# Summing edges with the one-hots as weights, two groups side by side in TensorE's column halves, then placing the sums

## The reference, cut to what matters

```
h = relu(layernorm(x))
agg = segment_sum(edge_attr, dst, 12500)          # 200000 x 48 -> 12500 x 48
z1 = silu(concat(h, agg) @ W1 + b1)               # 176 -> 256
z2 = silu(z1 @ W2 + b2)                           # 256 -> 256
out = x + h + z2 @ W3 + b3                        # 256 -> 128
```

## Time and profile before

| | |
|---|---|
| median of 3 runs | 367.58 us (367.41 to 370.16) |
| the profiled execution's own time | 369.57 us |
| its span, first to last instruction | 367.8 us |
| PE busy | 347.2 us (94%) |
| PE weight loads busy | 327.8 us (89%) |
| DVE busy | 260.8 us (71%) |
| ACT busy | 203.1 us (55%) |
| POOL busy | 32.6 us (9%) |
| data moved | 52.96 MB, 144 GB/s on average |

### The profile page before, as it was taken

How to read it: one execution, slowest core, us unless ns; L and a number is a source line. 1 busy time by engine, 2 the same in 40 slices (tenths; PEclk the granted TensorE clock), 3 DMA queues, 4 the chain that set the end, 5 groups by cost and what they waited for, 6 DMA issues and landing times.

```text
span 367.8 us, 11752 instructions
## 1 busy us (share of the span) xinstructions
PE 347.2 (94%) x4336; PEld 327.8 (89%) x4337; DVE 260.8 (71%) x630; ACT 203.1 (55%) x377; POOL 32.6 (9%) x44
## 2 busy tenths in 40 slices
PE   1488999999999999999999999999999999999995
PEld 1387999999999999999999999999999999999994
DVE  6864866976687667866796669766876688666652
ACT  7543466555655566456645565556555654566471
POOL 4011101110111001110111011101110011101100
PEclk9996999999999999999999999999999999999999
DMA  4953756454555455455635554545554555551111
GB/s 136 295 158 83 219 152 177 131 167 134 175 134 165 127 173 168 131 138 172 182 115 152 165 174 123 169 133 175 137 163 127 172 153 149 138 170 28 27 27 47
DMA packets 78757, 52.96 MB, mean 144 GB/s; under 512 B 2482, under 2 KB 78348, under 8 KB 78738
## 3 DMA queue, kind: packets, MB, share of 16 engines
q1 hardware_dynamic: 78738, 52.70, 50.3%
HBM read 46.29 MB, written 6.40 MB: 143 GB/s over the span
## 4 chain that ended last, share of the span: by engine, by line
PE 93%; DVE 4%; issue 2%; POOL 1%; ACTq 0%; DVEq 0%; POOLq 0%; ACT 0%
PE agg_ps L836 41%; PE z L899 14%; PE z L880 7%; PE z L888 6%; PE z L882 6%; PE z L869 3%; PE z L864 3%; PE z L870 3%; PE z L865 3%; PE z L866 3%; PE tp L849 3%; DVE farthest L522 1%; PE z L774 1%; DVE window L505 0%; DVE rel_rows L518 0%
## 5 line engine op out<-in xcount | busy, mean ns | idle before, releaser
L836 PEld LDWEIGHTS agg_ps<-onehot,raw 128*48 128x48 f32 x3128 | 147.8, 128 | 7.3 <-issue 3.6
L836 PE MATMUL agg_ps<-onehot,raw 128*48 128x42 f32 x3128 | 151.1, 217 | 3.3 <-issue 3.3
L714 DVE TENSOR_TENSOR out_t<-z,resid 112x512 f32<-112x512 f32 (+1 forms) x28 | 19.4, 692 | 84.6 <-PE z L899 84.6
L558 DVE TENSOR_TENSOR onehot<-window,rel 128x1176 f32<-128x1176 f32 (+1 forms) x56 | 76.9, 1375 | 0.7
L425 ACT ACTIVATE xn<-x_t,nmr,rstd 112x128 f32<-112x128 f32 (+1 forms) x112 | 46.2, 483 | 36.6 <-DVE nmr L550 29.8
L899 PEld LDWEIGHTS z<-w,h 128*112 128x112 f32 (+1 forms) x448 | 51.7, 176 | 5.3 <-issue 4.5
L377 POOL TENSOR_TENSOR rstd<-vareps,minus_half 112x4 f32<-112x4 f32 (+1 forms) x28 | 28.2, 1008 | 312.0 <-DVE vareps L542 312.0
L899 PE MATMUL z<-w,h 128*112 128x128 f32 (+1 forms) x448 | 54.4, 274 | 0.9 <-ACT h L446 0.9
L446 ACT ACTIVATE h<-z,b2c 128x448 f32<-128x448 f32 (+1 forms) x56 | 32.4, 631 | 26.5 <-PE z L888 26.5
L880 PE MATMUL z<-h_hi,w_hi 128*128 128x448 f32 (+1 forms) x112 | 43.5, 389 | 0.0
L385 ACT ACTIVATE agg_ps<-zeros 48x512 f32<-48x512 f32 x28 | 16.5, 592 | 45.4 <-DVE agg_carry L668 45.4
(11 more groups left out here) (89 smaller groups left out, 341.4 us busy)
## 6 DMA issues: line engine op xcount, KB each, us to landing
raw<-in_edge_attr_dram SPq DMA_DIRECT2D x55, 672.0 KB, 4.6
x_t<-in_x_dram SPq DMA_DIRECT2D x27, 224.0 KB, 2.9
out_dram<-out_t SPq DMA_DIRECT2D x27, 224.0 KB, 2.5
dst_rows<-in_dst_dram SPq DMA_DIRECT2D x1, 768.0 KB
raw<-in_edge_attr_dram SPq DMA_DIRECT2D x1, 480.0 KB, 4.0
out_t<-in_L_gnn_W_dram SPq DMA_DIRECT2D x1, 256.0 KB, 7.0
x_t<-in_x_dram SPq DMA_DIRECT2D x1, 192.0 KB
out_dram<-out_t SPq DMA_DIRECT2D x1, 192.0 KB
```

The source lines that it names most:

```text
L558: return dve.tensor_tensor(onehot[:, slot, 0:n * PER, :], window[:, :].unsqueeze(1).broadcast_to([P, n * PER, WINDOW]), cols.unsqueeze(2). ...
L836: mm = pe.matmul(banks[0:ED, bass.ds(offsets[k], WINDOW)], raw[0:rows, slot, k, j, :], onehot[0:rows, slot, k * PER + j, :], start=False, ...
```

## The change

The edges' sums are made in two stages.

First `sum_tile` multiplies with the **one-hot as weights** (128 x 42) and the **edges moving** (128 x 48). Its result is a group's 42 x 48 sums at a fixed place of one PSUM bank, `stage`: groups of even number on partitions 0 to 41, those of odd number on 64 to 105 (`tile_position=(0, 0)` and `(0, 64)`), 7 pairs of groups next to each other. No offset is needed for it. ScalarE copies the bank to SBUF (`stage_sums`, 106 x 336).

Then `place_batch` puts each group in its place: one fp32 multiplication with the staged sums (106 x 48) as weights and 42 columns of the identity as the moving operand, added into `agg_ps` at the group's offset, two pairs of load and matmul for each group. A batch is shifted by 3 groups against the tile: batch b places groups 14b-3 to 14b+10, so that the bank of tile b-1 is closed within it, and its offsets are read from entry 14b-3 on.

What goes with it: `stage` takes a bank, so that both layers now share one `z` (2 banks) in place of `z1` and `z2`, and `layer1` waits for `activate2` of the tile before, chunk by chunk. `layer2` is done chunk by chunk. TensorE's step becomes `layer1(i-1)`, `offsets_of(i+1)`, `sum_tile(i+1)`, `layer3(i-2)`, `transposes(i)`, `place_batch(i+1)`, `layer2(i-1)`. ScalarE's and VectorE's orders are rewritten, edges are loaded three tiles ahead into the same four slots, and one-hots are made two tiles ahead. The start is rearranged: the first entry of each group and the first 128 groups of `dst` are loaded ahead of the rest, tiles 0 and 1 are summed before the offsets of the other groups are known, and TensorE gets some matmuls of the identity whose results are not used.

The core of the diff:

```diff
-    LOOP_FIRST, LOOP_END = 4, 24
+    LOOP_FIRST, LOOP_END = 4, 22
+    WARM0, WARM1 = 10, 6
...
+        staged = sb("staged", [ROW2 + WINDOW, 2, PAIRS, ED])
...
-        z1 = ps("z1", [P, M, BANK])
-        z2 = ps("z2", [P, M, BANK])
+        stage = ps("stage", [P, BANK])
+        z = ps("z", [P, M, BANK])
...
             def step(i, parity):
-                if has(i, -2, NT):
-                    load_edges(i + 2, parity, 0)
+                if has(i, -3, NT):
+                    load_edges(i + 3, 1 - parity, 0)
...
+            def stage_sums(t, parity):
+
+                act.wait_ge(s_summed, 2 * t + 2)
+                if not isinstance(t, int) or t > 1:
+                    act.wait_ge(s_placed, t)
+                act.activation(staged[:, parity].rearrange("w k d -> w (k d)"), stage[0:ROW2 + WINDOW, 0:STAGED],
+                               ACT.Copy).then_inc(s_staged, 1)
...
             def step(i, parity):
                 if has(i, 1, NT):
                     relu(i - 1)
+                if isinstance(i, int) and i == 1:
+                    clear_carry(2)
+                if has(i, 1, NT):
+                    split_agg(i - 1)
                 if has(i, 1, NT - 2):
                     act.wait_ge(s_carried, i)
                     clear_bank(1 - parity)
-                if has(i, 1, NT):
-                    split_agg(i - 1)
-                if has(i, 0, NT):
-                    normalize(i, parity)
                 if has(i, 2, NT):
                     activate2(i - 2)
                 if has(i, 1, NT):
                     activate1(i - 1)
-
+                if has(i, 0, NT):
+                    normalize(i, parity)
+                if has(i, -1, NT):
+                    stage_sums(i + 1, 1 - parity)
...
-            def offsets_of(i):
-                count = sum(groups_of(i, half)[0] for half in range(2))
+            def batch_of(b):
+
+                t = isinstance(b, int)
+                first = 0 if t and b == 0 else -EARLY
+                last = sum(groups_of(b, half)[0] for half in range(2)) if t and b == NT - 1 else GPT - EARLY
+                return first, last
+
+            def offsets_of(b):
+                first, last = batch_of(b)
                 _, offsets = nc.values_load_multi_w_load_instructions(
-                    offset_row[0:1, bass.ds(i * GPT, count)], engines=[mybir.EngineType.PE],
+                    offset_row[0:1, bass.ds(b * GPT + first, last - first)], engines=[mybir.EngineType.PE],
...
+                    for j in range(PER):
+                        for side in range(2):
+                            half, k = divmod(2 * pair + side, HALF)
+                            if 2 * pair + side < total:
+                                rows = P if k < counts[half][1] else TAIL_P
+                                at = ROW2 * side
+                                mm = pe.matmul(stage[at:at + WINDOW, pair * ED:(pair + 1) * ED],
+                                               onehot[0:rows, 2 * parity + half, k * PER + j, :],
+                                               raw[0:rows, 2 * parity + half, k, j, :],
+                                               start=(pair == 0 and j == 0), stop=True, skip_group_check=True,
+                                               tile_position=(0, at))
...
+            def place_batch(b, parity, offsets):
+
+                first, last = batch_of(b)
+                pe.wait_ge(s_staged, b + 1)
+                wait(pe, s_clear, b + 1)
+                for offset, k in zip(offsets, range(first, last)):
+                    group = k % GPT
+                    at = ROW2 * (group % 2)
+                    mm = pe.matmul(banks[0:ED, bass.ds(offset, WINDOW)], staged[:, parity if k >= 0 else 1 - parity, group // 2, :],
+                                   ident[0:ROW2 + WINDOW, at:at + WINDOW],
+                                   start=False, stop=True, skip_group_check=True)
...
                 for m in range(M):
                     cols = slice(m * P, (m + 1) * P)
-                    pe.matmul(z1[:, m, 0:n], w1x_hi[:, cols], hT_hi[:, 0:n], start=True, stop=False)
...
+                    wait(pe, s_h2, M * (t - 1) + m + 1)
+                    pe.matmul(z[:, m, 0:n], w1x_hi[:, cols], hT_hi[:, 0:n], start=True, stop=False)
...
                     layer1(i - 1)
                 if has(i, -1, NT):
                     offsets = offsets_of(i + 1)
+                    sum_tile(i + 1, 1 - parity)
                 if has(i, 2, NT):
                     layer3(i - 2)
                 if has(i, 0, NT):
                     transposes(i, parity)
                 if has(i, -1, NT):
-                    sum_tile(i + 1, 1 - parity, offsets)
+                    place_batch(i + 1, 1 - parity, offsets)
                 if has(i, 1, NT):
                     layer2(i - 1)
 
-            sum_tile(0, 0, first_offsets)
+            pe.wait_ge(s_stage_clear, 1)
+            sum_tile(0, 0)
...
+            sum_tile(1, 1)
+            transposes(0, 0)
+            first_offsets = offsets_of(0)
+            offsets = offsets_of(1)
+            where_invalid(pe, mybir.EngineType.PE, general_path)
+            place_batch(0, 0, first_offsets)
+            place_batch(1, 1, offsets)
             pipeline(pe, step)
```

More of the change, by code:

```diff
@@ L113, in gnn_kernel @@
         centre_i = sb("centre_i", [P, ROWS], I32)
+        first_i = sb("first_i", [P, ROWS], I32)
         g = {n: sb("g_" + n, [P, ROWS]) for n in (
-            "base", "middle", "centre", "drift", "ok1", "ok2", "ok3", "valid", "invalid",
-            "tile", "tilet", "tile_half", "pair", "parity", "offset", "offset2", "offset3",
-            "at_centre", "instead", "placed", "shift")}
+            "base", "middle", "minus_middle", "centre", "tilet", "tile", "tile_half", "pair", "parity",
+            "begin", "in_tile", "at_centre", "other", "if_before", "if_behind", "from_centre",
+            "drift", "place", "before", "behind", "moved1", "moved2", "moved3", "ok1", "ok2", "ok3",
+            "valid", "invalid", "far", "chosen", "placed", "shift")}
         rel = sb("rel", [P, NG, PER])
@@ L237, in pipeline @@
         def pipeline(eng, step):
-            for i in range(LOOP_FIRST):
+            for i in range(1, LOOP_FIRST):
                 step(i, i % 2)
@@ L589, in _ @@
+            weights_lo()
             dve.wait_ge(s_rel, ROWS)
+            for half in range(2):
+                make_onehot(2, 0, half)
             def general_path():
@@ L621, in general_path @@
                 turn(0, gen_rel, g["ok1"], ALU.add)
[L622 removed]
+                dve.wait_ge(s_onehot, 6)
                 turn(1, rel, g["shift"], ALU.subtract)
[L625 to L626 removed]
+                dve.wait_ge(s_summed, 4)
                 before = chain[0]
@@ new lines, in sum_tile @@
+            def sum_tile(i, parity):
+                counts = [groups_of(i, half) for half in range(2)]
+                total = sum(n for n, _ in counts)
+                wait(pe, s_staged, i)
+                for pair in range(PAIRS):
+                    for k in (2 * pair, 2 * pair + 1):
+                        n, full = counts[k // HALF]
+                        slot = 2 * parity + k // HALF
+                        if k % HALF == 0:
+                            pe.wait_ge(s_edges[slot], 16 * slot_turn(i, parity) + (16 if full < n else 0))
+                            pe.wait_ge(s_onehot, 2 * i + k // HALF + 1)
+                    for j in range(PER):
+                        for side in range(2):
[8 more added lines that the diff above has]
+                                               tile_position=(0, at))
+                                if 2 * pair + side == HALF - 1 and j == PER - 1:
+                                    mm.then_inc(s_summed, 1)
+                mm.then_inc(s_summed, 1)
```

388 lines of the change are left out of this document (216 added, 172 removed).

## The result

| | before | changed |
|---|---|---|
| median | 368.34 us | 417.38 us (4 runs) |
| ratio | | 1.1303, 95% interval 1.1209 to 1.1398 |
| span of the profiled execution | 367.8 us | 413.9 us |
| PE busy | 347.2 us, 94% | 330.9 us, 80% |
| a step (layer 1 to layer 1), steps 2 to 26 | 12.00 us | 13.71 us, most often 13.39 |

One of the changed kernel's four executions was longer than the rest (426.41 us); it counts in the median and is left out of the ratio.

A forecast was written before the change was run, and what follows sets the result against it. TensorE, busy 94%, was taken as the bound. Step: 4.36 + 2.8 + 0.3 + 1.75 + 0.48 + 1.29 + 2.52 = 13.50 against 12.02 us; 367.8 + 38 - 5 = 401 us, median 400, range 338 to 445.

The forecast's parts named there:

- the likeliest case: Whole kernel: exposed register load, overlapping halves, step 13.50 us against 12.02; 386 to 412 us, chance 0.36.
- the rival with the falling clock: Steps: idle gaps lower the clock too; a 6.8 us fall costs about 3.4; 423 or 445 us, chance 0.13.
- The register load: Offsets' load behind layer 1: takes 3.36 us, ends at 4.36, leaving TensorE idle 2.33 us in each step.
- Every load should be long: Batches begin 4 or 12 bytes off 16, so each load takes 3.36 us; only starts on 16 bytes take 1.34.
- The lead of the sequencer: Sequencer runs some 17 pairs, about 3.5 us, ahead; a waiting matmul holds all behind it, register loads too.
- The sum: Edges' sum, 112 pairs in two column halves: 2.8 us at 25 ns a pair, 5.16 without overlap.
- emptying: Going over to halves and back may empty the array: 0 to 0.33 us a step, 0.3 taken.
- The start: Before the steps: first sums perhaps 8 us sooner, against uncovered placements and loads; 0 to 10 sooner, 5 taken.
- So nothing shows: SyncE's queue: x waits behind a load of edges held for `sum_tile(i+1)`, but is needed some 6 us later; no cost.
- The halves overlap: Sum's column halves overlap, 2.8 us; rival without overlap 461 us, half overlap 431, with exposed load chance 0.13.
- The faster case: Rival: register load short or covered, a gain below 1.9 us; 350 at 1.34, 341 covered, range 333 to 360, chance 0.32.

The follow-up runs named there:

- e2_shift: Changed kernel with the row of offsets written, and read from, one entry (4 bytes) later: 393.92 us in a single execution.
- e7_third_bank: Changed kernel with a third bank for `z`, so layer 1's second chunk no longer waits for ScalarE's second chunk of the tile before: 412.3 us, ratio 1.1201.
- e11_bank_x_first: `e7_third_bank` with x loaded ahead of the edges: 385.76 us, ratio 1.0481 to the kernel before.
- e4_both: Changed kernel with 16 entries for each batch in the row of offsets and the register load put ahead of layer 1: 348.45 us, ratio 0.9482.
- e8_start: `e4_both` with x loaded ahead of the edges, and the first two batches' offsets loaded before the other groups' tables are turned: 339.94 us, ratio 0.9231.
- e6_one_half: `e4_both` with odd groups summed in the same column half and PSUM partitions as even ones (sums mixed up): 408.08 us in a single execution.
- e3_aligned: Changed kernel with 16 entries for each batch in the row of offsets, the load left behind layer 1: 356.58 us, ratio 0.973.

## Why the prediction was right, step by step

The direction and the mechanism held: the long load behind layer 1's second wait. The forecast of 400 was 17 us short of the measured 417, and the result lies outside the likeliest case's own range (386 to 412), between it and the rival with the falling clock. Of the span, 401 were forecast and 413.9 profiled: the start is 5.5 us longer than was taken, the steps some 6, the end 1.2.

- **The register load.** "Every load should be long" held at 3.34, and the rule read from even and odd tiles (a start on 16 bytes) held when `e2_shift` turned the classes round. The stretch was put at 2.33 and is 2.62: the sum starts 0.3 behind the load's end, as layer 3 did in the kernel before (190.8 + 3.36 = 194.16 and 194.43), and that had been left out. The reads took 96 or 239 ns per register, by where they start. The 200 ns that the prediction takes from the Trainium skill ("Runtime: NRT & Kernel Launch") are given there for registers read from HBM, and this row lies in SBUF.
- **The lead of the sequencer.** It held. `e7_third_bank` with `e11_bank_x_first` shows it for two waits: the load follows the last of layer 1's waits to be met, whichever it is.
- **The sum.** 2.8 plus 0.3 for emptying; it took 2.52 with both changes of mode in it. The floor of 25 ns a pair isn't one between two halves (22.5), and hardly any emptying can be seen: where no load stands before it (`e4_both`), the sum starts 0.30 behind the start of layer 1's last matmul, where 0.2 is usual, and layer 3 follows the sum at once. Layer 3 takes 0.08 more and placement 0.10. Together the parts were 0.4 too dear, the idle stretch 0.3 too cheap, so the step came out right (13.50, measured 13.39) partly by two errors that cancel.
- **The start** was the step that failed. 5 us sooner were taken, and it came 0.5 later. The first sum did come 7.3 us sooner (11.66 against 18.96). Of the three waits behind it, 11.4 us in all, only the loads of 1.5 and 3.3 us were foreseen; 4.1 us for ScalarE ahead of the last tables and 2.2 for the normalized x were not. Nor was the clock: from 28 to 42 us it is granted at half (0.51), and the first two placements take 4.22 us and not 2.6. It fell at 27.9, behind the wait for x and 1.0 us before the idle stretch of the loads begins, and in `e8_start`, where that stretch is 0.43 us, it is low for 10.2 us all the same. So the loads didn't bring it down; what did wasn't tried.
- **The clock** was a rival with 3.4 us lost for a fall of 6.8. In the profiled execution it fell in four steps, for half as long each (3.4 us), at 1.2 to 1.6 us. With 5.5 us in those steps and its part in the start, it belonged into the sum and not beside it: the earlier trace rows had the case, 2.47 us idle.
- **x.** "So nothing shows" was wrong by 3.3 us of waits for agg's rest, which made four steps 3.5 us longer. SyncE loads x behind the first half of the edges in both kernels. Before, it issued x 4.1 us behind that load of 672 KB (199.66 and 203.80), and now 0.6 behind it (195.24 and 195.82), because that load waits for the sum and x stands behind it. So x lands in 5.4 us and not 2.9, and VectorE's statistics wait with agg's rest behind them. The queue was named and the time that x needs was put too low, because the order of VectorE behind x was not followed.
- **Rivals.** The halves overlap (`e6_one_half`). The faster case needed loads below 1.9 us, and with 1.34 it came (`e3_aligned`: 356.6, where 350 had been worked out). The Trainium skill ("TensorE: Matmul & The Clock Gate", Part 3, The mechanism) says that weight loads overlap matmuls in flight only in another row group; the trace doesn't agree for column halves, with 22.5 ns from pair to pair against 43.6 in one half. The Trainium skill ("TensorEngine Tiling (Array Packing)", Key Properties) says that tiles load weights and multiply in parallel, and the trace agrees; the drain that it names can be 0.1 us at most on the way in (0.30 against 0.2) and 0.08 on the way out (layer 3).

## What to carry to other kernels

A read of registers is an instruction of the sequencer: here it cost next to nothing as long as enough work was queued ahead of it, and 2.6 us of its 3.3 in each step as soon as a matmul ahead of it waited for another engine. When a buffer is shared to save a bank, look at what stands in the program behind the new wait, not only at whether the array would wait. And when a stretch of idle TensorE appears, look for the clock behind it before the sum is closed.

## What the runs showed of the hardware that was not expected

- A read of 14 registers takes 1.34 us from a start on 16 bytes and 3.34 from 4, 8 or 12 bytes off it. Started while placement is at work it takes longer: 3.9 to 4.4 for 3.34, and 1.6 to 2.6 for 1.34. Why wasn't settled.
- Two column halves, 42 columns of weights and 48 moving, fp32: 22.5 ns from pair to pair, 43.6 in one half.
- GpSimd's power of 112 x 4 numbers takes 2.06 us in the changed kernel and 1.01 before. It now runs beside a one-hot of VectorE (217.82 beside 217.68 to 219.06). That this is the cause was not tried.
